# Decoder layer on one core: a new order of the opening, FFN weights made ternary inside the first iterations, gates as column tiles

## The chip, the cores and the metric

One core of a Trainium2 chip. The metric is device time in microseconds, median of several runs. The core has five engines with instruction queues of their own: TensorE (PE, matmuls, with its weight loads shown as PEld), VectorE (DVE), ScalarE (ACT), GpSimd (POOL) and SyncE (SP, which here issues every DMA). Engines wait for one another through semaphores; every queue runs in the order in which it was written.

## The reference

Sixteen sequences of 256 rows and 256 features pass one decoder layer with post-norm:

```python
# attention, 16 heads of 16, with a bias that depends on the distance i - j
q, k, v = x @ Wq.T + bq, x @ Wk.T + bk, x @ Wv.T + bv
attn = softmax(q k^T / 4 + pos_bias[:, i - j + 255])
x = layernorm(x + (attn v) @ Wo.T + bo)
# gated linear memory, 4 heads of 64; keys and values are the context
ig, fg = concat(x, ctx, ctx) @ gate_kernels + biases     # 4 + 4 rows
D = exp(cs_i - cs_j + ig_j - running max)                # cs: cumsum of log_sigmoid(fg)
h = ((q k^T / 8 * D) / max(|row sum|, exp(-max))) @ v    # causal
x = layernorm(x + headnorm(h) * outnorm_scale)
# FFN 256 -> 1024 -> 256; weights rounded to -1, 0, 1 times mean(|w|), rows rounded to 8 bits
x = layernorm(x + bitlinear(silu(bitlinear(x, w_gate)) * bitlinear(x, w_up), w_down))
```

## The kernel before

All of one sequence (a batch) lies in SBUF as 2 x 128 rows. The program is unrolled: each engine has a function `body(b)` that is called for b = -2 and then, in `iterations`, for b = -1 to 19. Inside a body the steps of several batches are interleaved in an order written out by hand: n2 = b + 2 is projected to q and k, b (and the first heads of n = b + 1) goes through the softmax, c = b - 1 through the output projection, first norm and gates, f = b - 2 through memory heads and the first half of the FFN, e = b - 3 through the down projection, d = b - 4 is stored.

**Attention.** `q_proj` and `k_proj` (L648) give q and k turned, `q_copy` and `k_copy` (L1092, L1103) add the bias `bqk`. POOL splits each into three bf16 parts (`split_high` L414 and L416, `split_low` L425 and L427), and SP copies them in six DMAs each into the stacks `qs` and `ks` (`load_stack`, L299), of which one 96-row matmul per 128 queries makes the scores of a head (`scores`, L599). `parts` is written again only when the stack DMAs of the batch before have landed. DVE adds the position bias and finds the row maximum (`biased`, L1292; two per head), ACT and POOL subtract (`negated`, L935 and L437), PE turns four 128 x 128 blocks (`turned`, L615), ACT exponentiates (L947), and PE multiplies by v with four heads in four column tiles (`values`, L632). `pS` has two banks, so scores of a head wait for DVE on the head two before. `attention_residual` is L1604, once per batch.

**Gates and memory.** `mem_gates` (L761, L764) sums four matmuls of 68 output rows (input gates in 0 to 3, forget gates in 64 to 67). ACT makes `gate_rows` (L986 to L990) and `gate_logs`; DVE scans (`forget_sums`, `input_rows`, `running_max` L1568); SP writes the maxima to DRAM and reads them back to all 128 partitions (`save_max`, `spread_max`, tile `mb`); ACT (`mem_late`, `mem_weights`), POOL (`mem_causal`), DVE and PE do the heads. Three PSUM banks are passed round in the order of the list `uses`: `lease` makes a use wait until the one before it in its bank is read.

**FFN.** `gate_proj`, `up_proj`, `gate_tanh`, `gated`, `gated_up`; then each row is scaled and rounded (`scaled` on ACT, `inner_quantised` L449 on POOL), turned by a DMA transpose (`turn_inner`, L337, tile `th<-hq`) and multiplied by `wd` (`down`, L751).

**The opening.** SP issues the four attention weights, x of batch 0, five rows of 256 (bq, bk, bv, bo, norm) into one partition, gate weights and gate biases, the three FFN weights of 1 MB (L278, L280) and the position bias in four DMAs of 1 MB (L287: 2 query tiles x 16 heads x 256 columns per partition). The first wait of PE is for all four weights. DVE waits for all small loads (`d_small`), and copies the turned weights out of PSUM (L1242, L1245). PE spreads the rows over the partitions by matmuls with ones (L573 to L578), DVE copies them, and only then (V_BC) `body(-2)` starts: x of batch 0 is turned and q and k are projected. Then the FFN weights: sums of absolute values on DVE (L1256), the mean by a matmul with ones (L902), scaling on ACT (L1206), rounding to -1, 0, 1 on DVE (L1264, L1265), 48 transposes on PE (L914) and copies on DVE. PE waits for the last of these (V_ALL) and DVE for the whole position bias before `iterations`.

## Time and profile before

| | |
|---|---|
| time, median of 3 runs | 766.72 us (765.93 to 768.02) |
| profiled execution, its own time | 766.44 us |
| its span, first to last instruction | 764.6 us |
| mean granted TensorE clock | 0.933 |
| busy: PE, DVE, ACT, POOL | 640.8, 617.4, 597.5, 483.2 us |
| DMA | 68.32 MB, mean 89 GB/s |

The busy shares are means over three stages: an opening without scores, a beat that repeats once per batch, and an end in which only the last batch is left. A stage has to be read by itself, by windows and by the chain of waits in it.

### The profile page before, as it was taken

To read this page: it belongs to the slowest core of one execution; us is meant where nothing else is said; L and a number is where in the kernel's file an instruction comes from. 1 tells how busy PE (TensorE), PEld (TensorE's weight loads), DVE (VectorE), ACT (ScalarE), POOL (GpSimd) and SP (SyncE) were. 2 spreads that over 40 slices of the span, in tenths; PEclk is the share of its full clock that TensorE was granted. 3 is DMA by queue.
4 is the path that set the end of the run, shared out by engine and by line. 5 is a ranking of instruction groups with operands and counts; after the bars stand their busy time and mean duration, and the time that the engine had idled before them with its cause. 6 is when DMAs were issued, how large, how long until landed. Compare 5 with 4: busy or idle time off the path is not lost.

```text
span 764.6 us, 17069 instructions
## 1 busy us (share of the span) xinstructions
PE 640.8 (84%) x4882; PEld 476.4 (62%) x4912; DVE 617.4 (81%) x2261; ACT 597.5 (78%) x1253; POOL 483.2 (63%) x833
## 2 busy tenths in 40 slices
PE   4367997999999999999999999989999989785542
PEld 3345776667676758686868676867676757452311
DVE  2755464899999999999999999988999999875752
ACT  0415795999999998989898999988999989875421
POOL 2415654667777868787778777776777765535332
PEclk8587998999999999999999999999999999897855
DMA  8887624154445545454545453635353542120201
GB/s 266 156 143 111 97 60 74 23 114 65 123 74 112 83 113 84 111 84 112 84 111 84 109 87 89 95 85 101 70 117 60 108 59 72 42 56 15 69 15 41
DMA packets 96966, 68.32 MB, mean 89 GB/s; under 512 B 40229, under 2 KB 96618, under 8 KB 96874
## 3 DMA queue, kind: packets, MB, share of 16 engines
q1 hardware_dynamic: 96874, 67.23, 44.7%
q8 instruction: 41, 0.67, 0.4%
q14 instruction: 51, 0.42, 0.2%
HBM read 29.39 MB, written 4.26 MB: 44 GB/s over the span
## 4 chain that ended last, share of the span: by engine, by line
PE 28%; DMA 23%; ACT 13%; SPq 10%; DVE 10%; issue 10%; POOL 6%; POOLq 0%; ACTq 0%; DVEq 0%
DMA mb<-mrows 13%; DMA th<-hq 7%; SPq L299 6%; PE pT L615 3%; PE pO L632 3%; ACT L997 2%; PE pA L751 2%; ACT h L1124 2%; SPq L337 2%; DVE mm L1568 2%; PE pB L739 2%; DMA ks<-parts 2%; PE pB L764 1%; PE pB L761 1%; PE pS L599 1%
## 5 line engine op out<-in xcount | busy, mean ns | idle before, releaser
L1292 DVE CUSTOM_DVE_ANT_0 sc<-pS,bias 128x256 f32<-128x256 f32 x512 | 201.4, 416 | 28.0 <-PE pS L599 26.8
L947 ACT ACTIVATE pr<-pT 128x512 f32<-128x512 f32 x256 | 154.5, 608 | 22.0 <-PE pT L615 21.4
L615 PE MATMUL pT<-ident,sc 128*128 128x128 f32 x1024 | 153.1, 277 | 5.1 <-POOL sc L437 3.2
L437 POOL TENSOR_SCALAR sc<-sc,mx 128x256 f32<-128x256 f32 x256 | 123.3, 493 | 23.3 <-DVE mx L1292 20.8
L615 PEld LDWEIGHTS pT<-ident,sc 128*128 128x128 f32 x1024 | 119.6, 142 | 28.1 <-issue 17.1
L935 ACT ACTIVATE sc<-sc,mx 128x256 f32<-128x256 f32 x256 | 130.2, 516 | 3.0 <-DVE mx L1292 3.0
L599 PE MATMUL pS<-ks,qs 96*128 96x256 bf16 x512 | 93.8, 274 | 9.1 <-DVE mx L1292 6.5
L489 POOL TENSOR_SCALAR_AFFINE_SELECT mb<-mb 128x256 f32<-128x256 f32 x64 | 26.3, 411 | 80.2 <-ACT mb L974 79.2
L632 PE MATMUL pO<-pr,va 128*32 128x256 f32 x1024 | 70.2, 393 | 0.5 <-ACT pr L947 0.5
L599 PEld LDWEIGHTS pS<-ks,qs 96*128 96x128 bf16 x512 | 47.9, 98 | 34.0 <-DVE mx L1292 17.0
L449 POOL TENSOR_SCALAR hq<-h 128x512 bf16<-128x512 f32 x64 | 38.7, 620 | 32.0 <-ACT h L1124 31.8
L414 POOL TENSOR_SCALAR parts<-qk_f 128x512 bf16<-128x512 f32 x32 | 19.9, 621 | 56.0 <-ACT qk_f L1092 39.1
L751 PE MATMUL pA<-wd,th 128*128 128x256 bf16 x256 | 37.4, 295 | 19.4 <-DMA th<-hq 17.8
L1036 ACT ACTIVATE x<-y,shift,rs 128x256 f32<-128x256 f32 x64 | 34.7, 592 | 20.3 <-POOL shift L402 20.3
L632 PEld LDWEIGHTS pO<-pr,va 128*32 128x32 f32 x1024 | 27.1, 110 | 29.8 <-issue 9.7
L1488 DVE TENSOR_TENSOR h<-h,pA 128x512 f32<-128x512 f32 x64 | 43.7, 683 | 1.1 <-PE pA L706 0.7
L1304 DVE BATCH_NORM_STATS2 st<-y 128x6 f32<-128x256 f32 x96 | 36.0, 417 | 9.4 <-POOL y L505 9.3
L751 PEld LDWEIGHTS pA<-wd,th 128*128 128x128 bf16 x256 | 25.4, 104 | 28.9 <-issue 22.6
L1124 ACT ACTIVATE h<-h,magic,hs 128x1024 f32<-128x1024 f32 x32 | 39.5, 1236 | 4.6 <-DVE hs L1521 4.6
L391 POOL TENSOR_SCALAR ve<-mv 128x2 f32<-128x2 f32 x48 | 12.2, 254 | 48.7 <-DVE mv L1314 48.5
L416 POOL TENSOR_TENSOR qk_f<-qk_f,parts 128x512 f32<-128x512 f32 x32 | 41.2, 1287 | 2.7
L1292 DVE DVE_READ_ACCUMULATOR2_ANT mx<- 128x1 f32 x512 | 41.5, 81 | 0.0
(223 smaller groups left out, 1736.3 us busy)
## 6 DMA issues: line engine op xcount, KB each, us to landing
qs<-parts SPq DMA_DIRECT2D x96, 128.0 KB, 4.7
ks<-parts SPq DMA_DIRECT2D x96, 128.0 KB, 4.5
mb<-mrows SPq DMA_DIRECT2D x16, 512.0 KB, 7.5
xin<-in_x SPq DMA_DIRECT2D x16, 256.0 KB, 2.8
bias<-in_L_attn_pos_bias SPq DMA_DIRECT2D x4, 1024.0 KB, 20.8
xb<-in_x SPq DMA_DIRECT2D x16, 256.0 KB, 3.0
cx<-in_ctx SPq DMA_DIRECT2D x32, 128.0 KB, 2.1
out<-hq SPq DMA_DIRECT2D x16, 256.0 KB, 3.2
```

Of the source, the lines that this page charges most:

```text
L299: sp.dma_start(dst, src).then_inc(stack.sem, 16)
L416: pool.tensor_tensor(src, src, parts[:, 0, which, :, :], ALU.subtract).then_inc(split.sem, 1)
L437: pool.tensor_scalar(sc[:, s % RING, 1, :], sc[:, s % RING, 1, :], -1.0, mx[:, s % RING, 1:2], ALU.mult, ALU.add).then_inc(neg_g.sem, 1)
L599: ins = pe.matmul(pS[s % 2][:, t * S:t * S + S], qs[par][:, s, t * P:t * P + P], ks[par][:, s, :], start=True, stop=True)
L615: ins = pe.transpose(bank[:, kt * S + t * P:kt * S + t * P + P], sc[:, s % RING, t, kt * P:kt * P + P], ident[:])
L632: ins = pe.matmul(pO[32 * j:32 * j + 32, 0:S], va[par][:, kt, hd, :], pr[:, hd % RING, kt, :], start=(kt == 0), stop=(kt == TT - 1))
L751: ins = pe.matmul(bank[:, 0:D], hqT[:, t, j, :], wd[:, j, :], start=(j == 0), stop=(j == FT - 1))
L935: act.activation(sc[:, s % RING, 0, :], sc[:, s % RING, 0, :], ACT.Identity, bias=mx[:, s % RING, 0:1], scale=-1.0).then_inc(neg_a.sem, 1)
L947: act.activation(flat(pr[:, s % RING, :, :]), pT[s % 2][:, :], ACT.Exp, scale=-1.0)\
L1124: act.activation(h[:, t, :], h[:, t, :], ACT.Identity, bias=magic[:, :], scale=hs[:, 4, t:t + 1])\
L1292: dve.tensor_tensor_reduce(out=sc[:, s % RING, t, :], in0=pS[s % 2][:, t * S:t * S + S], in1=bias[:, t, s, ::-1], scale=1.0, scalar=LOW, o ...
L1488: dve.tensor_tensor(dst, dst, bank_of(f"u{i}")[:, :], ALU.mult).then_inc(h_v.sem, 1)
```

## The change

- **Order of the opening.** SP issues Wq, x of batch 0, Wk, then bq and bk element by element straight into `bqk`, the bias of heads 0 to 3, Wv, x of batch 1, the bias of heads 4 to 7, Wo, and bv, bo and the norm row by DMAs that repeat the row for all 128 partitions. The rows through PE and their copies on DVE are gone. After these come the q and k stacks of batch 0, the other two bias loads, the gate weights and the first FFN weight. PE turns Wq and Wk, does `body(-2)`, then turns Wv and Wo. k of batch 0 is split by DVE (`k_split`) instead of POOL.
- **Position bias held once.** 384 columns per head instead of 2 x 256; tile t reads from column 128 t.
- **FFN weights.** They are loaded one after the other into `h` (`stage`), column blocks first, in pieces of 512 bytes: `weight_sums`, `weight_mean`, `weight_inverse`, `weight_round`, `weight_signs` do in iterations 0 (w_gate), 1 (w_up) and 2 (w_down) what the opening did; a DMA transpose (`weight_turn`) writes the turned weight. `weight_mean` on PE writes into spare columns of `pO`, so `values` of three groups waits until DVE has read it.
- **Gates.** `gate_parts` puts four matmuls of 32 output columns into four column tiles, ACT copies the 128 rows (`gate_copy`), and one matmul with the 0/1 matrix `fold` adds the four parts and places the rows (`gate_sums`).
- **Orders.** The bodies of all engines and the list `uses` are ordered anew; the memory heads of c and the end of attention of b now stand at the end of body b instead of at the beginning of the next. SP issues both `turn_inner` of a batch before the ks stack; POOL splits q at the beginning of its body and the high part of k after negated(n, 0).

```diff
-            for i, w in enumerate((Wq, Wk, Wv, Wo)):
...
+            load_weight(0)
             sp.dma_start(xin[:, 0, :, :], x[0].rearrange("(t p) d -> p t d", p=P)).then_inc(x_in.sem, 16)
...
+            load_weight(1)
+            for i, r in enumerate((bq, bk)):
+                src = bass.AP(tensor=r.tensor, offset=0, ap=[[1, DH], [KT * DH, NH // KT], [DH, KT]])
+                sp.dma_start(bqk[:, i, :], src, allow_slow_non_contiguous=True).then_inc(d_qk.sem, 16)
+            load_bias(0)
+            load_weight(2)
+            sp.wait_ge(x_in.sem, 16)
+            sp.dma_start(xin[:, 1, :, :], x[1].rearrange("(t p) d -> p t d", p=P)).then_inc(x_in.sem, 16)
+            load_bias(1)
+            load_weight(3)
+            for dst, r in ((bv_bc, bv), (bo_bc, bo), (nw_bc, norm_w)):
+                sp.dma_start(dst[:], bass.AP(tensor=r.tensor, offset=0, ap=[[0, P], [1, D]])).then_inc(d_rows.sem, 16)
+
+            def weight_load(i):
+                if i:
+                    sp.wait_ge(wt_v.sem, 2 * i)
+                dst = stage.rearrange("p (a b c) -> p a b c", b=FT if i < 2 else KT, c=P)
+                src = (w_gate, w_up, w_down)[i].rearrange("(b p) (a c) -> a p b c", p=P, c=P)
+                for a in range(KT if i < 2 else FT):
+                    sp.dma_start(dst[:, a, :, :], src[a]).then_inc(d_wf.sem, 16)
+
+            def weight_turn(i):
+                sp.wait_ge(wt_v.sem, 2 * i + 2)
+                dst = (wg, wu, wd)[i][:, :, :].rearrange("p a b -> p (a b)").rearrange("p (g r) -> p g r", r=P)
+                sp.dma_start_transpose(dst, tern[i]).then_inc(d_wt[i].sem, 16)
...
-                turn_inner(d, 1)
                 save_max(f)
                 load_x(n2, par)
-                load_residual(c)
+                if b == 3:
+                    weight_turn(2)
                 spread_max(f)
                 load_stack(n, 1 - par, 0)
                 store(d)
+                turn_inner(e, 0)
+                if b == 2:
+                    weight_turn(1)
+                    weight_load(2)
                 load_ctx(c)
-                turn_inner(e, 0)
+                turn_inner(e, 1)
                 load_stack(n, 1 - par, 1)
-
+                if b == 1:
+                    weight_turn(0)
+                    weight_load(1)
+                load_residual(b)
...
+            def gate_parts(c):
...
+                for j in range(4):
+                    rows = cxT if j < KT else x1T
+                    ins = pe.matmul(bank[32 * j:32 * j + 32, 0:S], gate_w[:, 2 + j if j < KT else j - KT, :],
+                                    rows[:, j % KT, :], start=True, stop=True)
...
+                pe.matmul(bank[0:64 + XH, 0:S], fold[:, :], gt[:, :], start=True, stop=True).then_inc(gt_ps.sem, 1)
...
+            def gate_copy(c):
...
+                act.activation(gt[:, :], bank_of("gp")[:, 0:S], ACT.Copy).then_inc(gp_sb.sem, 1)
...
+            def weight_sums(i):
+                dve.wait_ge(d_wf.sem, 16 * (KT, 2 * KT, 2 * KT + FT)[i])
+                dve.tensor_reduce(w_abs[:, i:i + 1], stage, AX.X, ALU.add, apply_absolute_value=True).then_inc(ws_v.sem, 1)
...
+            def weight_signs(i):
+                dve.wait_ge(wr_a.sem, i + 1)
+                dve.tensor_scalar(stage, stage, MAGIC, 1.0, ALU.subtract, ALU.min).then_inc(wt_v.sem, 1)
+                dve.wait_ge(wt_v.sem, 2 * i + 1)
+                if i == 2:
+                    dve.wait_ge(d_wt[0].sem, 16)
+                dve.tensor_scalar(tern[i], stage, -1.0, None, ALU.max).then_inc(wt_v.sem, 1)
```

In DVE's body the sums of w_gate stand before head 4 of batch 1, its inverse before head 6, its signs before head 8; the sums of w_up between the two halves of head 15 of batch 1, its inverse and signs after head 3 of batch 2; the sums of w_down before head 10 of batch 2, its inverse inside head 13, its signs after head 14. `weight_mean` stands on PE before values(0, 3), after scores(2, 3) and before scores(2, 12).

## Rows read from the trace of the kernel before

**Rows 1.** Chain of waits, opening to 141 us: start us, us, engine, what

```profile
6.24 2.90 DMA gate_b<-in_L_xattn_fgate_bias
...
42.79 12.07 DMA ks<-parts
...
70.28 0.44 PE pT L615 x4
...
84.31 1.00 PE pO L632 x16
85.31 0.59 PE pT L615 x4
```

**Rows 2.** Timeline, opening: start us, us, engine, line, operation [idle before <-releaser]

```profile
7.30 1.09 PE L568 MATMUL pS<-ident,pr 128*128 128x128 f32 x4 [7.30 <-DMA pr<-in_L_attn_Wo]
...
9.30 14.34 SPq L287 DMA_DIRECT2D bias<-in_L_attn_pos_bias  x4
...
10.34 1.26 DVE L1242 COPY wqT<-pS 128x256 f32<-128x256 f32 x2
...
21.08 4.61 DVE L1256 TENSOR_REDUCE w_abs<-sc 128x1 f32<-128x2048 f32 x2
...
22.99 3.78 PE L648 MATMUL pC<-xT,wqT 128*128 128x256 f32 x8 [0.77 <-ACT xT L1083]
...
26.57 2.53 PE L648 MATMUL pB<-xT,wkT 128*128 128x256 f32 x8
...
29.86 4.07 ACT L1206 ACTIVATE sc<-sc,magic,w_inv 128x2048 f32<-128x2048 f32 x2
...
31.81 7.31 SPq L299 DMA_DIRECT2D qs<-parts  x6
32.08 1.36 DVE L1264 TENSOR_SCALAR sc<-sc 128x2048 f32<-128x2048 f32 x1 [2.39 <-ACT sc L1206]
...
33.48 2.06 DVE L1265 TENSOR_SCALAR h<-sc 128x2048 bf16<-128x2048 f32 x1
...
54.90 0.61 PE L599 MATMUL pS<-ks,qs 96*128 96x256 bf16 x4 [0.31 <-DMA ks<-parts]
...
59.62 1.15 POOL L416 TENSOR_TENSOR qk_f<-qk_f,parts 128x512 f32<-128x512 f32 x1
```

**Rows 3.** DMA view, 0 to 22 us, then 22 to 55 (first line)

```profile
DMA packets 6313, 5.51 MB, mean 250 GB/s; under 512 B 1724, under 2 KB 6057, under 8 KB 6313
...
pr<-in_L_attn_Wv SPq DMA_DIRECT2D x1, 256.0 KB, 4.3
...
DMA packets 5426, 5.29 MB, mean 160 GB/s; under 512 B 280, under 2 KB 5424, under 8 KB 5424
```

**Rows 4.** Timeline, DVE, line 1604: second and last of 16

```profile
133.80 0.69 DVE L1604 TENSOR_TENSOR y<-pB,xb 128x512 f32<-128x512 f32 x1 [1.07 <-PE pB L672]
...
687.36 0.69 DVE L1604 TENSOR_TENSOR y<-pB,xb 128x512 f32<-128x512 f32 x1 [1.06 <-PE pB L672]
```

**Rows 5.** Busy time in eleven periods, 173.39 to 611.09 us: sum, mean

```profile
sum 437.70, PE 413.77 PEld 313.20 DVE 404.84 ACT 402.82 POOL 327.85; mean PE 37.62 PEld 28.47 DVE 36.80 ACT 36.62 POOL 29.80
```

**Rows 6.** Waits by pair, 212 to 571 us: us, times, longest

```profile
PE pA L751 <- DMA th<-hq: 4.1, 8, 1.6
```

**Rows 7.** Chain of waits in steady state, 140 to 260 us

```profile
171.74 0.57 SPq L299
...
175.66 5.08 DMA th<-hq
...
182.56 0.86 PE pB L761 x4
183.42 0.88 PE pB L764 x4
```

**Rows 8.** Busy time by stretch: us, PE, PEld, DVE, ACT, POOL, clock, DMA, GB/s

```profile
75.00:95.00 20.00, 18.58 (x157) 14.47 (x158) 9.50 (x49) 13.36 (x30) 13.67 (x21) 1.00 0.62 91
```

**Rows 9.** Groups by line, whole span: busy us, mean ns

```profile
L957 ACT ACTIVATE oT<-pO 128x256 f32<-128x256 f32 x64 | 24.9, 389 | 7.4 <-PE pO L632 7.3
```

More of the change, by code:

```diff
@@ L299, in load_stack @@
                     sp.dma_start(dst, src).then_inc(stack.sem, 16)
+            def load_stack(n, par, which):
+                if live(n) and n > 0:
+                    send_stack(n, par, which)
             def load_x(n, par):
-                if live(n) and not (isinstance(n, int) and n == 0):
+                if live(n) and n > 1:
                     wait(sp, x_in, n - 1, 16)
@@ L405, in split_high @@
             def split_high(n, which):
-                if not live(n):
+                if not live(n) or n == 0 and which == 1:
                     return
@@ L855, in body @@
+                scores(b, 10, par)
                 v_proj(n)
-                scores(b, 8, par)
-                turned(b, 4)
-                scores(b, 9, par)
                 turned(b, 5)
-                down(e, 0)
-                ctx_turned(c)
-                scores(b, 10, par)
+                scores(b, 11, par)
+                x1_turned(c, 1 - par)
+                down(e, 1)
+                gate_parts(c)
                 turned(b, 6)
-                values(b, 0, par)
-                x1_turned(c, 1 - par)
@@ L866, in body @@
-                scores(b, 11, par)
-                down(e, 1)
+                gate_sums(c)
+                if b == 2:
+                    weight_mean(2, 8)
                 scores(b, 12, par)
                 turned(b, 7)
-                mem_gates(c)
                 scores(b, 13, par)
+                q_proj(n2)
                 scores(b, 14, par)
-                q_proj(n2)
+                k_proj(n2)
                 scores(b, 15, par)
                 turned(b, 8)
+                values(b, 0, par)
@@ L917, in _ @@
-            pe.wait_ge(v_set.sem, V_ALL)
+                up_proj(f, 2)
+                turned(b, 13)
+                values(b, 2, par)
+                up_proj(f, 3)
+                turned(b, 14)
+                mem_scores(c, 0)
+                turned(b, 15)
+                scores(n, 4, 1 - par)
+                scores(n, 5, 1 - par)
+                mem_values(c, 0)
+                mem_scores(c, 1)
+                mem_values(c, 1)
+                if b == 0:
+                    weight_mean(0, 3)
@@ L919, in _ @@
+                values(b, 3, par)
+            pe.wait_ge(g_set.sem, G_IDENT)
+            for k in range(4):
+                if k % KT == 0:
+                    pe.wait_ge(d_w[k // KT].sem, 16)
+                weight_turned(k)
+            body(-2)
+            for k in range(4, 8):
+                if k % KT == 0:
+                    pe.wait_ge(d_w[k // KT].sem, 16)
+                weight_turned(k)
+            pe.wait_ge(v_set.sem, V_VO)
             iterations(pe, body)
@@ L1089, in q_copy @@
                 act.wait_ge(pj_q.sem, pj_q.at(n, 1))
-                wait(act, split, n - 1, 4)
+                if n > 0:
+                    act.wait_ge(split.sem, split_at(n - 1, 4))
                 for m in range(KT):
@@ L1201, in _ @@
+                negated(n, 4)
+                exponentials(n, 2)
+                negated(n, 5)
+            act.wait_ge(v_set.sem, V_BIAS)
             act.wait_ge(g_set.sem, G_ALL)
             body(-2)
-            act.wait_ge(v_set.sem, V_ABS + 2)
-            for i in range(3):
-                act.activation(w_rows[i], w_rows[i], ACT.Identity, bias=magic[:, :], scale=w_inv[:, i:i + 1])\
-                    .then_inc(a_set.sem, 1)
             iterations(act, body)
```

607 lines of the change are left out of this document (313 added, 294 removed).

## The prediction

> **What bounds the kernel now.** I read the profile in this order: the chain of waits from the start, the timeline of the opening, the DMA view there, one DVE instruction that occurs once per batch, busy times by stretch, and waits by pair.
>
> The chain [rows 1] says that what ends last before the first scores is a DMA: ks<-parts, 12.07 us. The timeline [rows 2] shows why. PE's first scores stand at 54.90, but q of batch 0 left PE at 26.8 and k at 29.1; the six qs copies are issued at 31.8. Ahead of them SP issued four 1 MB bias loads over 14.34 us, behind 3 MB of FFN weights. From 22 to 55 us the queue moved 5.29 MB at 160 GB/s [rows 3]: it never ran dry. The FFN weight work of DVE, ACT and PE (21 to 47.6) lies inside that wait, so it costs nothing now. Projections start only at 21.1 since they follow a gate bias load (2.90 us, landed 9.14 [rows 1]), eight weight copies and three rounds of row broadcasts through PE.
>
> Afterwards the beat is read from L1604, once per batch [rows 4]: (687.36 - 133.80) / 14 = 39.5 us. In eleven such periods PE is busy 37.62, DVE 36.80, ACT 36.62 of 39.8 [rows 5]. Three engines are nearly full and no single one is the bound; the waits that remain are small. One of them is the transposed hq of the down projection, 0.5 us per period [rows 6], behind six ks issues of 0.6 us and a 5.1 us transfer [rows 7]. From the last L1604 to the end is a latency tail of 77 us.
>
> **The opening, step by step.** The new order is Wq, x0, Wk. The third 256 KB load stood at 1.80 and landed 4.3 us later [rows 2, 3]: Wk at 6.1. Four cold transposes, 1.09 [rows 2]: 7.2; x0 takes as many again (8.3) and a copy to SBUF, 0.7 with its gaps: 9.0. DVE's four copies (1.26 per weight) end at about 8.0 beside it. q projection 3.78: 12.8, k 2.53: 15.3 [rows 2]. From PE's q end (26.8) to SP's first qs issue (31.8) took 5.0: 17.8. Two stacks of six issues at 0.6 us [rows 7]: 25.2. k is split by DVE, four operations of about 0.7, beginning 16.2, ready 19 to 20, before SP gets to it at 21.5. Landing 5 us after the last issue, as the hq transfer does in steady state [rows 7]: 30.
>
> Is it full? Ahead of qs stand six loads of 256 KB, two bias loads of 768 KB (four heads, 384 columns, instead of 256 twice) and three of 128 KB: 3.5 MB. At 250 GB/s this is 14 us, at 160 GB/s 22 us [rows 3], so drained at 15.5 to 23.5. In the bad case the stacks (1.5 MB) need 10 us more: 33.5. The element-wise q and k bias (2 x 256 elements of 4 bytes) has no row; the nearest is the 16-byte gate loads with the gate bias behind them, landed in 2.90 us [rows 1]: bound 2 to 6 us after issue at 2.3 to 2.8, that is 4 to 9, hidden up to 9.0 where q's chain asks for it. I take first scores at 31, bounds 29.5 to 36: **-24**, from -25.4 to -19.
>
> The Trainium skill (DMA: Bandwidth & Descriptors, Rules for kernel authors) says a non-contiguous last dimension lowers to one descriptor per element and should be rearranged, which speaks against these bias loads. The row of the gate loads bears 2.9 us, so here it would stay hidden; by the rule, at several times that, the first scores would come some 5 us later.
>
> POOL then splits q of batch 1 once ks of batch 0 has landed, before and after. Before, the high split of k (a subtraction of 1.15 and a copy of half of that, 1.9 with gaps) also stood before negated(0, 0) [rows 2]; now behind it: **-1.9**, bounds 0 to -3 (PE is the chain right after).
>
> **FFN weights inside iterations 0 to 2.** Per matrix: sums 2.3 us DVE, rounding 2.03 ACT, signs 1.36 + 2.06 DVE (the first two are rows of two matrices, [rows 2]), plus small steps 0.3. That is 6 us DVE and 2 us ACT each, 18 and 6 in all; six PE transposes and copies fall away, replaced by three DMA transposes. How much shows?
> - Matrix 0 comes in iteration 0, where DVE is busy 9.50 of 20 us but PE 18.58 [rows 8]. PE waits in order at weight_mean(0) and at values(0, 3) until DVE did sums, heads (1, 4), (1, 5) and the inverse; behind them stand heads_turned and all scores. 3 to 5 us, take 4.
> - Matrix 1: PE waits less, 2 heads. Take 2.
> - Matrix 2 comes in iteration 2, where most of a full period's DVE work is present (36.80 of 39.8, [rows 5]): less slack than the 6 us added; take 4.
> - SP: in iteration 2 weight_turn(1) waits for DVE's signs, and load_ctx(1) is queued behind it and eight loads of 0.5 us issue each. ctx is wanted at ctx_turned(1), some 15 us later. 0 to 5, take 2. In iteration 3 spread_max(1) stands behind weight_turn(2). 0 to 3, take 1.
>
> Sum **+13**, bounds +4 (everything in idle time) to +22 (all of DVE's 18 and ctx).
>
> **Steady state.** Gates: PE had 0.86 + 0.88 = 1.74 per batch [rows 7]. Now four matmuls in four column tiles, half of a values call (16 rows, 1.00): 0.5, and one sum matmul, a quarter of 1.74: 0.45. After a values call the next four transposes take 0.59 where others take 0.44 [rows 1], so 0.15 for the change of tiling. Net 1.74 - 1.10 = -0.64 PE. ACT gains one PSUM copy of 256 columns, 0.39 as its copy of pO of that shape [rows 9]: 36.62 to 37.0. A wait is added: PE at gate_sums waits for this copy with only four transposes between; behind it stand scores 12.
>
> The Trainium skill (TensorEngine Tiling (Array Packing), Key Properties) says that changing the tiling mode drains the TensorE. The trace agrees to the extent of the 0.15 above; the sum by it is the same.
>
> All orders are new as well. Both turn_inner now precede the ks stack, which takes 6 x 0.6 us out from ahead of a transfer that PE waits for (4.1 us in nine periods, [rows 6]); running_max stands two heads earlier, so mb arrives earlier against mem_late. Sum of such waits: about 1 us per period. DVE, unchanged at 36.8 plus its in-order gaps, limits the gain; the floor is near 38.3 (-1.2), and the ceiling is a worse order, +0.8. I take -0.6 for 13 periods: **-8**, bounds -16 to +10.
>
> The tail: mem and FFN of the last batch stay the same chain; the gates gain a copy and lose a sum: 0, bounds -3 to +3.
>
> **Sum** against the profiled execution (766.44; its span is 764.6 and the median 766.72, so nothing to shift): 766.4 - 24 - 1.9 + 13 - 8 = **745.5**.
>
> **Rivals.**
> - *The beat does improve.* The period falls to 38.3 and the weight work costs 8 instead of 13: 766.4 - 24 - 2 + 8 - 16 = 732. For: three engines with 2 to 3 us of waits. Against: no engine but PE loses work.
> - *The opening is given back.* Weights cost 20 and the period stays: 766.4 - 24 - 2 + 20 = 760. For: PE, in order, carries the chain through iterations 0 and 1. Against: DVE's idle half there.
> - *The DMA queue keeps the stacks.* Bias runs and broadcasts at 160 GB/s hold qs to 36 and more; the gain is 19 and the rest as above: 750.
> - *Slower.* The new gate step makes a cycle: gate_sums waits for ACT, which is late by an exponential (0.6) or more, scores 12 come late, so DVE and then ACT. At +1.5 us per period (41.0) times 14 it costs 21: 766.4 - 26 + 13 + 21 = 774. It decides from about +1 us per period. For: ACT has become the fullest engine with DVE. Against: the copy is asked for just behind negated(b, 11), and ACT waited 2 to 3 us per period already.
>
> **How the numbers follow.** Chances: forecast (738 to 753) 0.40, better beat (722 to 738) 0.22, stacks late 0.10, opening given back (753 to 764) 0.18, slower 0.06, and 0.04 for what lies beside these. The range runs from 726 to 763. A measurement of this kernel can tell 0.3%, 2.3 us: faster 0.89, same 0.04, slower 0.07.
>
> **What would show it.** First scores at 29.5 to 33 with ks landing just before; L1604 of batch 0 22 us earlier than before; its first three distances longer than 39.5 by some 2, 6 and 1; later distances near 39. PE waits for DVE w_mean before values(0, 3). The gates' PE time falls to 1.1. It is wrong if the first scores come after 36, if the sum of DVE's and ACT's weight steps falls into idle time, or if the distances after the fourth batch are not between 38.3 and 39.6.

## The result, and the profile after

The changed kernel takes 771.04 us (median; 768.64 to 776.99), the kernel before 766.36 in the same sessions: ratio 1.0064, 95% interval 1.0047 to 1.0082. It is slower, by 0.6% and clear of the interval; 745.5 was predicted, with a range of 726 to 763. The profiled execution has a span of 769.9 us (before 764.6) at a mean granted clock of 0.916 (before 0.933).

attention_residual (L1604 before, L1694 after) cuts both executions at the same places:

| stretch | before, us | after, us | difference | predicted |
|---|---|---|---|---|
| start to the first one | 94.61 | 76.14 | -18.5 | -21.9 |
| its first three distances | 118.13 | 127.63 | +9.5 | +9 |
| the other twelve | 474.62 | 489.02 | +14.4 | -8 |
| the last one to the end | 77.2 | 77.1 | -0.1 | 0 |

(Of the 13 us that the prediction gave the FFN weights, 4 lie in iteration 0, ahead of the first attention_residual; so the first stretch is -24 - 1.9 + 4.)

The opening is as it was meant to be. Timeline of after, SP's queue and PE (start us, us, engine, line, operation, idle before):

```profile
18.79 3.86 SPq L314 DMA_DIRECT2D qs<-parts  x6
22.70 3.88 SPq L314 DMA_DIRECT2D ks<-parts  x6
...
28.53 3.83 SPq L393 DMA_DIRECT2D gate_b<-in_L_xattn_igate_bias  x1
...
33.83 1.03 PE L638 MATMUL pS<-ks,qs 96*128 96x256 bf16 x4 [3.50 <-DMA ks<-parts]
```

The first scores start at 33.83 where they stood at 54.90 [rows 2], with ks landing just before.

The loss is in the steady state. Busy time by stretch of after (us, PE, PEld, DVE, ACT, POOL, granted clock, DMA share, GB/s): batch 0 to 1, 1 to 2, 2 to 3, and then nine periods:

```profile
76.14:115.71 39.57, 33.32 (x267) 25.17 (x265) 26.75 (x112) 31.59 (x70) 20.89 (x35) 0.96 0.67 146
115.71:163.84 48.13, 40.21 (x302) 28.62 (x301) 42.59 (x143) 40.09 (x83) 28.56 (x45) 0.89 0.43 78
163.84:203.77 39.93, 37.22 (x306) 27.90 (x305) 37.84 (x142) 37.14 (x80) 30.84 (x52) 1.00 0.51 92
244.70:613.22 368.52, 346.15 (x2738) 259.38 (x2737) 343.77 (x1252) 334.90 (x712) 277.38 (x460) 0.96 0.51 91
```

Beside them one such period of the kernel before:

```profile
371.50:410.70 39.20, 37.67 (x302) 28.50 (x303) 36.91 (x139) 36.61 (x79) 29.77 (x52) 1.00 0.49 92
```

Read the nine periods against it and [rows 5]: a period is 40.95 us, DVE's busy time has gone up from 36.8 to 38.2 although its work in these periods is the same, and the granted clock is 0.96 where before it is 1.00. Only the third distance is at 1.00, and it is 39.93. (The probe kernel below, which is the changed kernel up to its last work, has two such distances, 39.90 and 40.06.) So a full-clock period of the changed kernel is no shorter than before, and the ten that follow it, at 0.96, are 0.9 to 1.3 us longer. The lower clock is no accident of one execution: its mean is 0.912 to 0.927 over the 20 runs, and 0.931 or more in every run of the kernel before that stands beside the experiments.

The waits of after in those nine periods (us in total, times, longest) and PE's timeline in one of them show where. xq is the quantised input of the FFN, and `rows_turned` is the step of PE that turns it:

```profile
PE pB L624 <- DVE xq L1557: 16.6, 9, 1.9
...
POOL nrm L516 <- DVE nrm L1479: 8.0, 10, 1.0
```

```profile
462.85 1.07 PE L673 MATMUL pO<-pr,va 128*32 128x256 f32 x16
465.76 0.38 PE L624 MATMUL pB<-ident_b,xq 128*128 128x128 bf16 x4 [1.84 <-DVE xq L1557]
466.10 0.42 PE L638 MATMUL pS<-ks,qs 96*128 96x256 bf16 x2
466.32 1.06 PE L654 MATMUL pT<-ident,sc 128*128 128x128 f32 x4
```

```profile
464.00:469.00 5.00, 3.24 (x16) 2.15 (x17) 4.77 (x17) 4.39 (x9) 4.59 (x8) 0.73 0.14 40
```

PE reaches rows_turned and waits 1.84 us for DVE's xq; right behind it four transposes take 1.06 us instead of 0.60, and the granted clock of the stretch is 0.73: part of it at 1.2 GHz instead of 2.4. The wait was 0.29 us before:

```profile
386.17 0.38 PE L585 MATMUL pA<-ident_b,xq 128*128 128x128 bf16 x4 [0.29 <-DVE xq L1467]
```

Why is xq late? DVE's and POOL's timelines of after, side by side, hold part of the answer:

```profile
422.04 1.64 POOL L554 TENSOR_TENSOR xb<-xb,bo_bc 128x512 f32<-128x512 f32 x1
...
446.44 1.16 POOL L465 TENSOR_TENSOR parts<-qk_f,parts 128x512 bf16<-128x512 f32 x1
```

```profile
421.65 0.95 DVE L1642 TENSOR_TENSOR_SCAN cs<-gt,sp 4x256 f32<-4x256 f32 x1
422.64 1.06 DVE L1546 SCALAR_TENSOR_TENSOR fs<-fs,w_gu,minus_half 128x2 f32<-128x2 f32 x1
...
446.72 0.90 DVE L1447 TENSOR_TENSOR nrm<-nrm,emT 128x8 f32<-128x8 f32 x1
```

The same two operations before:

```profile
384.48 0.31 DVE L1456 SCALAR_TENSOR_TENSOR fs<-fs,w_gu,minus_half 128x2 f32<-128x2 f32 x1
...
369.17 0.19 DVE L1357 TENSOR_TENSOR nrm<-nrm,emT 128x8 f32<-128x8 f32 x1
```

L1546 (row_factors) works on two elements per partition and takes 1.06 us; it took 0.22 or 0.31 before. It ends at 423.70, POOL's residual_in at 423.68. L1447 (head_bound) takes 0.90 instead of 0.19 and ends at 447.62, POOL's split_low at 447.60. Each ends within 0.02 us of the POOL instruction beside it. (residual_in has grown too, from 1.28 to 1.64 us; it starts beside the scan L1642.) The other part is order: forget_sums' scan (L1642) and input_rows now stand ahead of xq, 1.6 us; before, they stood behind it.

### The profile page after: what moved, and what is told of

The parts are those of the page before. It is cut to its first block, busy times and chain, and to the rows that moved or that the text cites. A ratio compares the mean times of both kernels' runs of the same rounds, so it can differ in the third digit from the quotient of the medians.

```text
span 769.9 us, 17096 instructions
## 1 busy us (share of the span) xinstructions
PE 647.6 (84%) x4892; PEld 471.1 (61%) x4892; DVE 630.4 (82%) x2259; ACT 606.6 (79%) x1269; POOL 494.1 (64%) x829
## 4 chain that ended last, share of the span: by engine, by line
PE 25%; ACT 24%; DVE 21%; issue 17%; POOL 8%; SPq 2%; DMA 2%; POOLq 0%; DVEq 0%; ACTq 0%
ACT pr L1006 5%; DVE sc L1382 4%; PE pT L654 4%; ACT mb L1033 3%; ACT x L1105 3%; ACT sc L994 3%; POOL nrm L518 3%; ACT th L1195 2%; PE pB L624 2%; PE pS L638 2%; ACT mb L1025 2%; PE pC L802 2%; PE pA L755 2%; PE pC L740 2%; PE pO L673 2%
## 5 line engine op out<-in xcount | busy, mean ns | idle before, releaser
L654 PE MATMUL pT<-ident,sc 128*128 128x128 f32 x1024 | 161.1, 285 | 6.0 <-issue 3.2
L1006 ACT ACTIVATE pr<-pT 128x512 f32<-128x512 f32 x256 | 150.2, 593 | 18.5 <-PE pT L654 17.6
L654 PEld LDWEIGHTS pT<-ident,sc 128*128 128x128 f32 x1024 | 123.7, 146 | 28.1 <-ACT sc L994 8.1
L475 POOL TENSOR_SCALAR sc<-sc,mx 128x256 f32<-128x256 f32 x256 | 128.0, 511 | 12.7 <-DVE mx L1382 11.4
L994 ACT ACTIVATE sc<-sc,mx 128x256 f32<-128x256 f32 x256 | 124.5, 506 | 10.0 <-DVE mx L1382 9.9
L638 PE MATMUL pS<-ks,qs 96*128 96x256 bf16 x512 | 102.5, 289 | 11.2 <-DVE mx L1382 7.5
L489 POOL TENSOR_SCALAR hq<-h 128x512 bf16<-128x512 f32 x64 | 38.6, 621 | 37.1 <-ACT h L1203 37.1
L624 PE MATMUL pB<-ident_b,xq 128*128 128x128 bf16 x64 | 6.7, 233 | 43.5 <-DVE xq L1557 43.5
L1382 DVE DVE_READ_ACCUMULATOR2_ANT mx<- 128x1 f32 x512 | 41.2, 81 | 0.0
L1586 DVE TENSOR_REDUCE hs<-h 128x1 f32<-128x1024 f32 x32 | 38.8, 1213 | 0.1
L465 POOL TENSOR_TENSOR parts<-qk_f,parts 128x512 bf16<-128x512 f32 x31 | 37.1, 1196 | 2.6
L454 POOL TENSOR_TENSOR qk_f<-qk_f,parts 128x512 f32<-128x512 f32 x31 | 36.4, 1175 | 2.6
```

The costliest lines, as they stand in the source:

```text
L465: pool.tensor_tensor(parts[:, 2, which, :, :], src, parts[:, 1, which, :, :], ALU.subtract)\
L475: pool.tensor_scalar(sc[:, s % RING, 1, :], sc[:, s % RING, 1, :], -1.0, mx[:, s % RING, 1:2], ALU.mult, ALU.add).then_inc(neg_g.sem, 1)
L489: ins = pool.tensor_scalar(hq[:, t, j * 512:j * 512 + 512], h[:, t, j * 512:j * 512 + 512], 1.0, -MAGIC, ALU.mult, ALU.add)
L638: ins = pe.matmul(pS[s % 2][:, t * S:t * S + S], qs[par][:, s, t * P:t * P + P], ks[par][:, s, :], start=True, stop=True)
L654: ins = pe.transpose(bank[:, kt * S + t * P:kt * S + t * P + P], sc[:, s % RING, t, kt * P:kt * P + P], ident[:])
L994: act.activation(sc[:, s % RING, 0, :], sc[:, s % RING, 0, :], ACT.Identity, bias=mx[:, s % RING, 0:1], scale=-1.0).then_inc(neg_a.sem, 1)
```

## The experiments

Some words first. A ring is a chain of waits over several engines that comes back to its start one period later and so sets the period. A hold is the time by which a DVE operation is longer because POOL's operation beside it is not over. The period is read at equal clock: "39.92 at 1.00" is a distance of attention_residual whose granted clock is 1.00. Each ratio is to the kernel before on the same chip.

**Quantisation ahead of the gates' rows, ACT alone.**

```diff
+                quantised(f)
...
                 gate_logs(c)
                 q_copy(n2)
-                quantised(f)
```
(and gate_rows(c) one place later, behind normed(f, 1))

> The changed kernel, with ACT's order alone edited: normed(f, 1) moved ahead of gate_rows(c), and quantised(f) ahead of gate_logs(c) and q_copy(n2), as in the kernel before. Theory late quantisation: in the changed kernel PE stands 1.84 us in every period at rows_turned until DVE has xq, because ACT makes the gate rows, the logs and the q copy first, and PE's granted clock is at 0.73 in the 5 us that follow; with the edit the gap shrinks below 0.6 us, the clock stays at 1.00 and the period falls from 40.9 to 39.5 or less, 13 periods or 18 us: 750 to 756. Theory gate tiles (the copy and the wait added to the gates make the cycle): the gates come 1.2 us later than in the changed kernel, the period stays at 40.9 or grows to 42: 770 to 785.

779.5 us, ratio 1.0177 (1.0113 to 1.0241). The last twelve distances are 40.5 to 41.8. DVE now waits at forget_sums, which stands in its order ahead of row_factors:

```profile
DVE cs L1642 <- ACT sp L1066: 30.0, 10, 3.0
```

With it row_factors is back at 0.26 us and the three late distances at clock 1.00 are still 40.5, so the hold on row_factors is not the only way to a long period.

**rows_turned two steps later on PE.**

```diff
-                rows_turned(f)
                 scores(n, 0, 1 - par)
                 turned(b, 9)
+                rows_turned(f)
```

> The changed kernel, with PE's order alone edited: rows_turned(f) moved behind scores(n, 0) and turned(b, 9). Theory that the gap on PE and the fall of its clock cost the time: PE has 0.65 us of work in the gap of 1.84, the stretch without work is 1.2 us, the clock may stay at 1.00, and the gate projections behind it take 0.43 us each instead of 0.85: 0.8 us per period, some 10 us in all, 758 to 764. Theory that the chain of latencies through xq sets the period and the clock is only its mark: rows_turned starts at the same time or later, period 40.6 to 41.2, 768 to 774.

791.21 us, ratio 1.0346 (1.0299 to 1.0394); the late distances are mostly 41.7 to 43.4, at 0.92 to 0.96. PE then waits 2.2 us per period for DVE in scores. Put behind other work of PE, the wait moves and gets longer. This fits a ring through xq, rows_turned and what follows.

**The gates as before, all new orders kept.** One accumulating group of four matmuls instead of column tiles, copy and sum:

```diff
-                    ins = pe.matmul(bank[32 * j:32 * j + 32, 0:S], ..., start=True, stop=True)
+                    ins = pe.matmul(bank[0:64 + XH, 0:S], ..., start=(j == 0), stop=(j == 3))
...
-                gate_sums(c)
...
-                gate_copy(c)
```

> The changed kernel with the gates of the kernel before: four matmuls of 68 output rows accumulated in one bank at the place of gate_parts, without the copy on ACT and the sum matmul. All orders are those of the changed kernel. Theory gate tiles: the period falls back by 1.2 us, 753 to 758. Theory late quantisation: PE does 0.5 us more and ACT 0.39 less, the chain from x1 to the gate rows is as long as it was (1.74 against 1.8 us), so the period stays within 0.3 us of 40.9: 767 to 775.

776.63 us, ratio 1.0152 (1.0112 to 1.0193): the column tiles aren't the cause, and without them the kernel is slower still. Nine of its late distances are at clock 1.00 and yet 40.7 to 41.1, 0.8 us above the full-clock period of the changed kernel. The rival on which the forecast of 774 rested, a cycle through gate_sums, falls. PE's wait for xq in one of the nine:

```profile
346.56 0.38 PE L624 MATMUL pB<-ident_b,xq 128*128 128x128 bf16 x4 [2.29 <-DVE xq L1555]
```

It is longer than the 1.84 us of the changed kernel, and the clock stays at 1.00. The length of this wait alone therefore doesn't decide on the clock.

**The weight steps on 16 columns.**

```diff
-                dve.tensor_reduce(w_abs[:, i:i + 1], stage, ...)
+                dve.tensor_reduce(w_abs[:, i:i + 1], stage[:, 0:16], ...)
```
(the same in the rounding and in the first step of the signs)

> The changed kernel with the FFN weight steps cut to 16 columns: the sums of absolute values and the first rounding step on DVE and the scaling on ACT touch 16 of 2048 columns; the last step (the maximum with -1, which writes the bf16 weight), all waits, loads and transposes stay. The weights are therefore not ternary. It takes away about 2.2 + 2.0 + 1.4 us per matrix. Theory that this work lies on the path in the first three iterations: the distance from batch 1 to batch 2 falls from 48.1 by 5 to 7 us and the total by 7 to 12: 759 to 764. Theory that it fills idle time: at most 3 us, 768 to 771. Periods from batch 3 on stay at 40.9 in both.

761.66 us, ratio 0.9942 (0.9916 to 0.9967): the length of these steps costs 9.4 us by the medians, of which the first three distances show 9.4 (118.27 against 127.63) and the stretch ahead of them 1.0. The third distance is 39.89 at 1.00 and the next ones 40.8 to 41.2 at 0.96, as with full steps; they leave nothing behind. Iteration 2, the second distance, is still 44.29.

**The opening and the weight steps alone, in the old orders.**

```diff
                 scores(b, 5, par)
+                if b == 1:
+                    weight_mean(0, 3)
...
                 biased(b, 14, 1)
+                if b == 2:
+                    weight_signs(2)
```
(and so on; the bodies, lifetimes and gates are otherwise those of the kernel before)

> The opening of the changed kernel and its weight steps inside iterations 0 to 2, but the body orders of all five engines, the data lifetimes and the gates of the kernel before; the weight steps hang at the nearest places of those orders. Theory (the new orders make the longer period): late distances of attention_residual go back to 39.6 from 40.9, the first residual stays near 76, the first three distances cost some 10 us in sum: 764.6 - 18.5 + 10 = 756 of span, ratio 0.987 (0.982 to 0.992). Rival (opening or weight steps leave something behind, such as a later start of the loads, that lengthens every period): late distances stay at 40.9 and the time is 768 to 772, ratio 1.002 to 1.007.

774.56 us, ratio 1.0115 (1.0079 to 1.0151). The total was missed: hung into the old orders, the weight steps cost 22 us in the first two distances (44.99 and 56.0 against 39.19 and 39.59), where they cost 8.9 us in the new ones. That part of the new orders is worth 13 us. The period is what the theory said: ten of the last twelve distances are 38.6 to 40.2 (39.6 in the mean). Two are 42.5 and 42.6, and both have a lower clock, behind a wait of 1.9 and 2.2 us for the transposed hq where their neighbours wait 0.8 to 1.4:

```profile
218.33:257.81 39.48, 37.55 (x302) 28.44 (x303) 36.67 (x139) 36.50 (x79) 29.79 (x52) 1.00 0.57 94
257.81:300.45 42.64, 39.19 (x302) 29.54 (x303) 37.00 (x140) 36.62 (x79) 29.56 (x52) 0.96 0.52 87
```

**POOL's residual_in away from row_factors.** First alone, then with split_low(n2, 1) away from head_bound:

```diff
+                residual_in(b)
                 output(e)
...
-                residual_in(n)
                 negated(n, 12)
```

```diff
                 split_high(n2, 1)
+                split_low(n2, 1)
                 mem_causal(c, 0)
```

> The changed kernel with one POOL step, residual_in (1.64 us), moved from ahead of negated(n, 12) to the start of the next body, away from DVE's row_factors. Theory (a small DVE operation with two SBUF tensors waits for the end of the POOL operation beside it): row_factors, 1.06 us now, falls to about 0.3 and, as it is in the ring, the period falls by 0.5 to 0.8 from 40.9: 759 to 763 of span against 769.9, ratio to before about 0.995. Rival (the two ends fall together by chance): row_factors stays near 1 us and the period within 0.2.

> As the previous kernel, and POOL's split_low(n2, 1), whose subtraction (1.16 us) runs beside DVE's head_bound (0.90 us instead of 0.19), moved to directly behind split_high(n2, 1). Theory of the wait for POOL's end: head_bound falls to about 0.2 and the period by another 0.4 to 0.7, to 39.5 to 40.0: 748 to 756 of span, ratio about 0.985. If the ring is held by something else, the period stays where the previous kernel has it.

762.86 us, 0.9967 (0.994 to 0.9994), and 759.64 us, 0.9914 (0.9882 to 0.9947). row_factors falls to 0.26, head_bound to 0.19, as foretold, and PE's wait for xq from 1.9 to 1.0 to 1.2. The way the gain comes was not foretold: distances are 39.9 to 40.1 at 1.00, just the one full-clock distance of the changed kernel. What changes is how many of the last twelve keep the clock at 1.00: none in the changed kernel, five in the first of these, ten in the second.

That the full-clock distance doesn't fall is no proof that the holds cost nothing, for the new place of residual_in makes another one. It now runs beside running_max's scan, which takes 1.40 us in both kernels; in the changed kernel it takes 0.67. POOL's and DVE's rows of the second kernel, then DVE's of the changed one:

```profile
336.35 1.76 POOL L554 TENSOR_TENSOR xb<-xb,bo_bc 128x512 f32<-128x512 f32 x1
...
337.25 1.40 DVE L1658 TENSOR_TENSOR_SCAN mm<-am 4x256 f32<-4x256 f32 x1
...
425.01 0.67 DVE L1658 TENSOR_TENSOR_SCAN mm<-am 4x256 f32<-4x256 f32 x1
```

**Both orders of the quantisation.** As the first experiment, with DVE's row_factors and quantised_rows ahead of forget_sums and input_rows too:

```diff
-                forget_sums(c)
                 row_factors(f)
-                input_rows(c)
+                biased(b, 14, 1)
                 quantised_rows(f)
-                biased(b, 14, 1)
...
+                forget_sums(c)
+                input_rows(c)
```

> The changed kernel with the quantisation of the FFN's input ahead of the gates' logarithms on both engines: ACT does normed(f, 1) and quantised(f) before gate_rows and gate_logs, DVE does row_factors and quantised_rows before forget_sums, input_rows and running_max. Theory (the ring passes quantised_rows, and the new order put 1.9 us of gate work ahead of it there: x2 norm to xq 6.1 us against 4.2 before): the period falls by 0.5 to 1.2 to about 40: 752 to 762 of span, ratio 0.985 to 0.995. Rival (the gates' rows then come late for mem_weights and the ring closes through them): period 40.9 or more, as where ACT alone was reordered (41.3), ratio 1.005 to 1.02.

784.53 us, ratio 1.0231 (1.0184 to 1.0279). PE then waits 2.7 us per period for ACT's pr, and two of the last twelve distances are at clock 1.00. So the early scan can't simply be put back: with the quantisation ahead of it another link is late.

**The weight signs behind max_rows in iteration 2** (on the kernel with both POOL steps moved):

```diff
-                if b == 2:
-                    weight_signs(2)
                 running_max(c)
...
                 max_rows(c)
+                if b == 2:
+                    weight_signs(2)
```

> The changed kernel with both POOL steps moved (759.64 us when last run, iteration 2 47.72 us), and weight_signs(2) (3.4 us of DVE) moved in iteration 2 from ahead of running_max to behind max_rows. Theory (iteration 2 is long because running_max, and with it mem_weights of batch 1 and scores of batch 3, stands behind the signs): iteration 2 falls by 2 to 3.4 us, to 44.5 to 45.7, and the time to 756.5 to 758. Rival (DVE is simply over-full there, the order does not matter): iteration 2 stays within 1 us of 47.7 and the time within 1 us of 759.6.

759.9 us, ratio 0.9893 (0.9857 to 0.9929); iteration 2 is 48.0. The rival held.

**A probe of DVE beside POOL,** behind the last work: POOL runs a tensor_tensor of two SBUF tensors, or a tensor_scalar of one, and DVE a small test operation.

```diff
+                        dve.tensor_scalar(sc[:, 0, 0, :], pS[0][:, 0:S], 1.0, 0.0, ALU.mult, ALU.add)
+                        test()
```

> The changed kernel with a probe behind its last work; its added time is of no interest. POOL runs either nothing of size, a tensor_tensor of two SBUF tensors (128x512, 1.28 us in the kernel) or a tensor_scalar of one (128x512, 0.61); beside each DVE runs one 128x256 operation from PSUM and then a test operation: tensor_tensor 128x2 of two SBUF tensors, tensor_scalar 128x2 of one, tensor_tensor 128x2 of PSUM and SBUF, tensor_tensor 128x256 of two SBUF tensors; all twice. Theory: beside the two-tensor POOL operation the 128x2 test of two SBUF tensors ends with it (0.6 to 0.9 us instead of 0.16), as does the 128x256 one (1.0 or more instead of 0.4), while the tests with one SBUF tensor or with PSUM keep 0.16 to 0.25. Rival (POOL slows every small DVE operation): all 128x2 tests are stretched alike.

Timelines, POOL's, then DVE's tests beside its 1.26 us operation: two SBUF tensors, one SBUF tensor, PSUM and SBUF, and 128x256 of two SBUF tensors:

```profile
779.18 1.26 POOL L607 TENSOR_TENSOR probe_p<-wqT,wkT 128x512 f32<-128x512 f32 x1 [0.51 <-DVE probe_d L1858]
...
782.57 1.26 POOL L607 TENSOR_TENSOR probe_p<-wqT,wkT 128x512 f32<-128x512 f32 x1 [0.51 <-DVE probe_d L1858]
```

```profile
778.64 0.15 DVE L1837 TENSOR_TENSOR probe_d<-bqk,minus_half 128x2 f32<-128x2 f32 x1
...
779.34 1.12 DVE L1837 TENSOR_TENSOR probe_d<-bqk,minus_half 128x2 f32<-128x2 f32 x1
...
782.73 1.13 DVE L1840 TENSOR_SCALAR probe_d<-bqk 128x2 f32<-128x2 f32 x1
...
786.13 0.15 DVE L1843 TENSOR_TENSOR probe_d<-pS,minus_half 128x2 f32<-128x2 f32 x1
...
789.68 1.39 DVE L1846 TENSOR_TENSOR sc<-bias 128x256 f32<-128x256 f32 x1
```

The first row is without a POOL operation: 0.15. Beside it the same takes 1.12 and ends at 780.46, POOL at 780.44. The theory was too narrow: a test of a single f32 SBUF tensor is held too (1.13), one that reads PSUM and SBUF isn't (0.15), and the 128x256 filler from PSUM kept its 0.42. POOL's shorter tensor_scalar (0.62) holds for 0.47 to 0.49. The Trainium skill (SBUF — State Buffer, SBUF: two separate sides) describes a pair of ports shared by VectorE and GpSimd as an exclusive lock: a DVE operation needs it in a 2-port mode, or with two SBUF inputs against a GpSimd operation that reads SBUF, and the later one is blocked until the other ends. All four tests agree, and the memset below does too.

**The mirror on the kernel before.** residual_in ahead of negated(b, 10):

> The mirror of the runs on the POOL steps: the kernel before, with residual_in (1.28 us) moved on POOL from behind split_high(n2, 1) to ahead of negated(b, 10), so that it runs beside DVE's row_factors (0.31 us there). Theory (a small DVE operation with two SBUF tensors lasts until the POOL operation beside it ends, and it is in the ring): row_factors rises to 0.9 to 1.2, the late distances of attention_residual rise from 39.5 by 0.3 to 0.9, the time from 766 to 770 to 778, ratio 1.005 to 1.016. Rival (the longer period of the changed kernel comes from its other orders, and the POOL step only adds to them there): the distances stay within 0.2, ratio 0.998 to 1.003.

841.74 us, ratio 1.0944, and it says nothing on the hold: row_factors kept 0.22 us, since POOL stood still until xb had landed, with all its later steps behind it:

```profile
POOL xb L514 <- DMA xb<-in_x: 71.8, 8, 9.8
```

**The hold or POOL's order.** Into the old place of residual_in, on the kernel with both steps moved, an operation of about its length that nobody needs: a memset, or a sum of two SBUF tensors.

```diff
                 negated(n, 11)
+                pool.memset(extra[:, :], 0.0)
```
(in the second kernel pool.tensor_tensor(extra[:, :], w0, w1, ALU.add))

> The changed kernel with both POOL steps moved (759.64 us, row_factors 0.26, late distances 39.92), and in the old place of residual_in, ahead of negated(n, 12), an added POOL memset of 128x1408 into a tile that nobody reads (about 1.3 us from 0.96 us for 128x1024): it delays POOL as residual_in did, but reads nothing from SBUF. Theory (what cost time there was the hold on DVE's small operations, not POOL's order): row_factors stays near 0.3, late distances within 0.3 of 39.9, time 758 to 763. Rival (the later negated(n, 12) cost the time): distances 40.3 to 40.7 with row_factors at 0.3, time 765 to 771.

> As the previous kernel, but the added POOL operation is a tensor_tensor 128x512 of two SBUF tensors (1.26 to 1.28 us), also into a tile that nobody reads. Theory (hold): row_factors rises to 0.7 to 1.1, late distances to 40.3 to 40.9, time 764 to 772, which is 5 to 10 us above the kernel with the memset. Rival (POOL's order): the same time as with the memset, within 2 us.

770.24 us, ratio 1.004 (1.0017 to 1.0062), and 777.9 us, ratio 1.0139 (1.0104 to 1.0174). Groups of DVE over 320 us (busy us, mean ns), memset, then two tensors:

```profile
L1567 DVE TENSOR_SCALAR xq<-att 128x512 bf16<-128x512 f32 x8 | 5.3, 664 | 0.1
...
L1556 DVE SCALAR_TENSOR_TENSOR fs<-fs,w_gu,minus_half 128x2 f32<-128x2 f32 x8 | 1.8, 221 | 0.3
```

```profile
L1558 DVE SCALAR_TENSOR_TENSOR fs<-fs,w_gu,minus_half 128x2 f32<-128x2 f32 x8 | 8.4, 1056 | 0.3
```

and PE's waits in one period of each:

```profile
PE pB L798 <- DVE cT L1642: 1.7, 1, 1.7
PE pB L634 <- DVE xq L1567: 1.1, 1, 1.1
```

```profile
PE pB L636 <- DVE xq L1569: 1.8, 1, 1.8
PE pB L800 <- DVE cT L1644: 1.7, 1, 1.7
```

Both theories get a share. In both kernels running_max's scan is back at 0.67, so they differ from the kernel with both steps moved by more than the added operation; from each other they differ by it alone. The memset takes the full-clock period from 39.92 to 40.52 though row_factors keeps 0.22: PE waits 1.7 us for cT instead of 0.5; that this is POOL's later mem_causal is argued, not shown. The two-tensor operation takes it to 41.24: row_factors 1.06, and PE's wait for xq 1.8 again. By the times the hold is worth 7.7 us (777.9 - 770.24), by the full-clock periods 0.7 each. The 10.6 us from 759.64 to 770.24, medians of two sessions, hold POOL's later work and more, less the hold on the scan that went away; the runs don't part them. (The memset doesn't spare everything: it holds the one-tensor xq, 0.66 instead of 0.41.)

The two-tensor kernel also shows two equal periods at unequal clock:

```profile
247.19:288.43 41.24, 38.05 (x304) 28.42 (x305) 37.00 (x139) 37.31 (x81) 31.97 (x53) 0.96 0.50 91
...
329.78:371.02 41.24, 36.87 (x304) 27.91 (x305) 36.83 (x139) 37.24 (x81) 31.95 (x53) 1.00 0.58 87
```

PE is busy 1.2 us longer in the first, and its wait for cT is 0.85 instead of 1.72. Here a later wait of PE took up what the clock cost.

**residual_in in a gap of POOL,** ahead of mem_causal(c, 3), where POOL waited 1.38 us for ACT and DVE reads PSUM; then without the move of split_low:

```diff
                 mem_causal(c, 2)
+                residual_in(b)
                 mem_causal(c, 3)
...
-                residual_in(n)
```

> The changed kernel with both POOL steps moved, and residual_in not at the start of the body, where running_max's scan beside it takes 1.41 us (1.04 in the kernel before), but ahead of mem_causal(c, 3), where POOL waits 1.38 us for ACT and DVE reads PSUM. Theory: the scan falls to 0.7 to 1.05; it is not in the ring that sets the period (mb comes early enough), so the distances fall by 0 to 0.4 from 39.92 and the time is 753 to 760. Rival (residual_in now delays mem_causal(c, 3) and with it cT in the ring): distances rise by 0.2 to 0.8, 762 to 770.

> The changed kernel with only residual_in moved ahead of mem_causal(c, 3); split_low(n2, 1) stays beside head_bound. It tells what each of the two moves of the fastest kernel (747.97 us) gives. If head_bound's hold (0.90 instead of 0.19 us) is in the ring: distances at clock 1.00 are 0.3 to 0.7 above 38.5, time 752 to 757. If only residual_in mattered: 38.5 at clock 1.00, time 746 to 750.

747.97 us, ratio 0.9755 (0.9715 to 0.9795), and 753.58 us, 0.9843 (0.9808 to 0.9878). The first was better than either theory allowed: 38.51 at 1.00, with running_max's scan down from 1.40 to 0.67 and no wait of PE for cT. With split_low beside head_bound it is 39.16:

```profile
240.40:279.56 39.16, 36.77 (x304) 27.88 (x305) 37.10 (x142) 36.79 (x80) 30.50 (x52) 1.00 0.55 95
```

The kernel of 753.58 us differs from the changed one by the place of residual_in alone, that of 747.97 us by split_low's too, and the scan takes 0.67 in both. So at full clock the places of the two steps are worth 0.77 us (39.93 to 39.16) and 0.65 us (39.16 to 38.51), about what row_factors and head_bound had grown by. A move takes away a hold and changes POOL's order at once; only the two runs with an added operation part the two, for row_factors. Two neighbouring periods of the first kernel show the price of the clock alone:

```profile
277.27:317.37 40.10, 38.16 (x304) 28.42 (x305) 36.49 (x139) 37.21 (x81) 30.57 (x52) 0.96 0.54 94
317.37:355.88 38.51, 36.57 (x304) 27.89 (x305) 36.07 (x139) 36.80 (x81) 30.50 (x52) 1.00 0.54 97
```

**The same step in the kernel before.**

```diff
+                residual_in(c)
                 mem_causal(f, 3)
...
-                residual_in(b)
```

> The kernel before, with its residual_in (1.28 us on POOL) moved in the same way as in the fastest kernel, ahead of the last mem_causal. There POOL waits 1.0 us for ACT before mem_causal anyway, PE's wait for xq is 0.29 us and the clock is at 1.00 in every late period. Theory (the step only costs where it holds DVE or delays POOL inside the ring, and the new orders brought it there): no gain, ratio 0.997 to 1.003. Rival (the step is simply worth 1.4 us per period wherever it leaves that run of POOL): distances fall by 0.5 to 1.4, ratio 0.975 to 0.99.

766.51 us, ratio 1.0012 (0.9985 to 1.0038). The cost of this step belongs to the new orders.

**scores(n, 0) ahead of rows_turned,** on the fastest kernel:

```diff
-                rows_turned(f)
                 scores(n, 0, 1 - par)
+                rows_turned(f)
```

> The fastest kernel (periods of 38.51 us at a granted clock of 1.00, of 40.10 at 0.96, four of the late ones) with scores(n, 0) ahead of rows_turned on PE instead of behind it: 0.2 us of work taken into PE's wait for xq, 1.04 us. Theory (a shorter wait keeps the clock): no late period at 0.96, time lower by 3 to 6 us, 742 to 745. Rival (the clock falls for another reason, or scores(n, 0) waits for DVE there): as many periods at 0.96, time within 2 us of 748 or above it.

746.53 us, ratio 0.9746 (0.9715 to 0.9776), the fastest kernel of this study. One distance of the steady state is at 0.96 (40.10), where the kernel without this move has four; the others are 38.5 to 38.7. But the wait didn't get shorter. PE now waits in scores, for DVE, in the periods at either clock:

```profile
255.42 0.38 PE L638 MATMUL pS<-ks,qs 96*128 96x256 bf16 x2 [1.38 <-DVE mx L1382]
```

That is 1.38 us against 1.04 at xq before the move. The time differs by less than the intervals, and four and one are counts of one profile each. The run doesn't test whether a shorter wait keeps the clock.

## Why the prediction was wrong, step by step

- **First scores (-24, bounds -25.4 to -19): right mechanism, -21.1.** ks landed at about 33.8, inside the 29.5 to 36, not at 30. q left PE at 13.5 instead of 12.8 and qs was issued at 18.79 instead of 17.8; ks landed 7 us after its last issue instead of 5. The element-wise bq and bk landed 3.1 and 2.9 us after their issue and did not hold the chain. Between the first scores and attention_residual it took 42.3 us, 39.7 before: +2.6, where the prediction has +4 for the first weight and -1.9 for POOL's k split. With short weight steps it is 41.3; the -1.9 by itself can't be seen.
- **FFN weights (+13, bounds +4 to +22): right in size.** In the three distances it was +9.5 for 9 predicted, and the run with short steps gives 9.4 back. The division was off: +0.4, +8.5, +0.6 instead of 2, 6 and 1. The second distance has 42.6 us of DVE work and an SP transpose of 3.26 us ahead of spread_max. How much of its remaining excess (44.3 with short steps) is whose stays open; the order of the signs has no part.
- **Gates (-0.64 of PE): right.** From first start to last end at full clock their matmuls take 1.89 us before and 0.64 + 0.62 after, and PE is busy 37.2 (36.6 in the kernel of 748 us) against 37.6 to 37.7. The rival that made them a cycle fell. Its 774 lies near the 771 by luck.
- **Orders (-8, bounds -16 to +10): the step that failed.** It said "DVE, unchanged at 36.8" and took a "ceiling" of +0.8 per period; measured is +14.4 in twelve periods, and DVE at 38.2. Durations had been taken as a property of an operation; here they depend on what the other engine runs beside it. row_factors grew by 0.8 and head_bound by 0.7, and the runs that took POOL's two steps away from them gave 0.77 and 0.65 us of a full-clock period back. (A third operation, in head_moments, grew by 0.4; others shrank.) PE's wait at rows_turned became 1.84 us instead of 0.29; without the hold on row_factors it is 1.04 to 1.2, and that the rest comes from the scan now ahead of xq is argued, not shown. The second part is the granted clock, which was in no term of the sum: it fell in each of the last twelve periods, 1.0 us a period here. It came back in most periods when the two steps stood elsewhere, so it goes with these places; why it falls in one period and not in the next stays open, and a wait of 2.29 us with the clock at 1.00 speaks against the length of PE's wait as the whole reason.
- **What was right in it:** the orders could pay. The floor "near 38.3" was nearly reached, with 38.51, once two steps of POOL stood elsewhere, and 746.5 to 748 is near the forecast (745.5). That is no merit of the forecast: it missed the changed kernel by 25 us, and outside its range.
- **Tail (0): right, -0.1.**

All five orders were new, and the prediction didn't ask which instructions of DVE and POOL meet in them.

## What to carry to other kernels

When an order is changed on POOL or DVE, lay the two timelines side by side and look for short DVE operations that end where a POOL instruction ends: on a ring they can cost what they have grown by in every period. A step moved away from one of them can land beside the next, as residual_in did beside the scan, so look again after the move. Compare periods at equal granted clock, and give the clock a line of its own in the sum: here it was 1.0 of the 40.9 us. A long POOL operation that nobody waits for did best here where POOL itself waited and DVE read PSUM.

## What the runs showed of the hardware

- A DVE operation that reads two SBUF tensors, or one f32 tensor from SBUF to SBUF, stands until the running POOL operation on SBUF tensors ends: 0.15 to 1.12 us for 128x2, 0.41 to 1.39 for 128x256. An operation with an operand in PSUM doesn't (0.15). A scan of 4x256 beside residual_in took 1.40 instead of 0.67. A POOL memset held the one-tensor xq (0.66) but not the two-tensor row_factors (0.22).
- The granted clock fell for a few microseconds behind PE's wait for xq of 1.84 us in the last twelve periods of the changed kernel, and behind waits of 1.0 to 1.2 us in some periods of the kernels with moved POOL steps. It did not fall behind 1.84 us in the third distance of the changed kernel (39.93 at 1.00), nor behind 1.8 us in six late periods with the added two-tensor operation (41.2 to 41.4 at 1.00), nor behind 2.3 us in nine with the gates as before (40.7 to 41.1 at 1.00). What decides was not found.
- What a period at 0.96 costs against one at 1.00 of the same execution was 1.6 us (38.51 and 40.10), 1.0 (39.93 and 40.94, the changed kernel), 0.2 (39.91 and 40.11, both POOL steps moved) and nothing (41.24 and 41.24, two-tensor operation). In the last two PE's wait for cT got shorter by 0.5 and 0.9 us.
- Two DMAs of four single elements each (gate_b) kept SP's queue for 3.83 and 2.78 us at issue, six copies of a stack for 3.86. A transpose DMA of wd took 3.26 us of issue. bq and bk, 256 single elements each, took 0.71 and 0.60 and landed 3.1 and 2.9 us after issue.
